# Moving one rotation behind a scaling and two low parts on VectorE in an attention kernel

## The reference, cut to what matters

```python
q = (x @ w_q); k = (x @ w_k); v = (x @ w_v)      # 32, 8 and 8 heads of 128
lq = x @ w_lq; lk = (lq @ w_lk); lv = (x @ w_lv) # 32 latent heads
q, k, lk = rope(q), rope(k), rope(lk)            # y * cos + rotate_half(y) * sin
attn = causal_softmax(q, repeat(k, 4)) @ repeat(v, 4)
lat  = causal_softmax(q, lk) @ lv
x = x + attn @ w_o + lat @ w_lo
x = x + ffn(layernorm(x))
```

## Time and profile before

| | us |
|---|---|
| median of 3 executions (lowest, highest) | 2121.59 (2121.29, 2122.29) |
| the profiled execution | 2121.26 |
| its span in the trace | 2119.5 |
| busy: TensorE, its weight loads | 2066.4, 1754.4 |
| busy: VectorE, ScalarE, GpSimd | 1531.2, 1203.0, 894.4 |

### The profile page before, as it was taken

The page is one execution under the profiler, slowest core; times in us unless marked ns, Lnnn a source line. Parts: engine busy times, 40 slices in busy tenths (PEclk is TensorE's granted clock), DMA queues, the critical chain, the costliest instruction groups (busy, mean ns, idle before and its releaser), DMA issues.

```text
span 2119.5 us, 32469 instructions
## 1 busy us (share of the span) xinstructions
PE 2066.4 (97%) x11236; PEld 1754.4 (83%) x11236; DVE 1531.2 (72%) x2946; ACT 1203.0 (57%) x2507; POOL 894.4 (42%) x691
## 2 busy tenths in 40 slices
PE   6999999999999999999999999999999999999989
PEld 5888888888888888888888888888888888888877
DVE  7777777776777677777677767777677777777775
ACT  4566555565566555566556555556646555555641
POOL 4433453444544353444443345444354345444411
PEclk9999999999999999999999999999999999999999
DMA  2111111111111111111111111111111111111121
GB/s 97 42 37 38 45 32 40 29 42 47 31 34 40 33 41 37 36 42 32 37 42 37 35 47 32 27 42 37 47 31 37 42 27 47 31 42 36 38 51 40
DMA packets 101937, 83.72 MB, mean 39 GB/s; under 512 B 28296, under 2 KB 73992, under 8 KB 101776
## 3 DMA queue, kind: packets, MB, share of 16 engines
q1 hardware_dynamic: 101776, 81.65, 15.1%
HBM read 79.26 MB, written 2.36 MB: 39 GB/s over the span
## 4 chain that ended last, share of the span: by engine, by line
PE 69%; DVE 15%; POOL 6%; issue 6%; ACT 4%; DMA 0%; SPq 0%; ACTq 0%; DVEq 0%
PE scores L433 9%; PE scores L435 9%; PE scores L434 9%; PE bankT L496 7%; PE bankX L433 6%; PE bankX L435 6%; PE bankX L434 6%; PE bankO L433 5%; PE bankO L435 5%; PE bankO L434 5%; DVE rot_half L1008 4%; DVE rot_half L1007 4%; DVE PT_lo L997 2%; POOL rot L1219 2%; POOL rot L1221 2%
## 5 line engine op out<-in xcount | busy, mean ns | idle before, releaser
L721 ACT ACTIVATE PT_hi<-bankT 128x512 fp32r<-128x512 f32 (+2 forms) x640 | 336.3, 532 | 389.1 <-PE bankO L435 326.9
L997 DVE TENSOR_TENSOR PT_lo<-bankT,PT_hi 128x512 fp32r<-128x512 f32 (+2 forms) x640 | 386.7, 607 | 194.7 <-ACT PT_hi L721 189.7
L780 ACT ACTIVATE probs<-probs,nmax 128x128 f32<-128x128 f32 (+7 forms) x512 | 395.5, 774 | 134.3 <-DVE nmax L991 133.7
L991 DVE CUSTOM_DVE_ANT_0 probs<-scores,mask 128x128 f32<-128x128 f32 (+7 forms) x512 | 381.3, 750 | 55.5 <-PE scores L435 54.4
L496 PE MATMUL bankT<-ident,probs 128*128 128x128 f32 x2304 | 379.1, 273 | 22.2 <-DVE PT_lo L997 20.0
L496 PEld LDWEIGHTS bankT<-ident,probs 128*128 128x128 f32 x2304 | 285.2, 140 | 90.6 <-DVE PT_lo L997 35.6
L1213 POOL TENSOR_TENSOR OT_lo<-o_raw,OT_hi 128x512 fp32r<-128x512 f32 x64 | 99.9, 1561 | 417.6 <-ACT OT_hi L721 417.6
L1219 POOL TENSOR_TENSOR rot<-rot,cos 128x512 f32<-128x512 f32 x144 | 186.2, 1293 | 199.4 <-DVE rot_half L1008 199.4
L721 ACT ACTIVATE OT_hi<-o_raw 128x512 fp32r<-128x512 f32 x128 | 147.0, 1148 | 145.5 <-DVE o_raw L1062 145.5
L1221 POOL TENSOR_TENSOR rot<-rot,rot_half 128x512 f32<-128x512 f32 x144 | 204.1, 1417 | 11.3
L1007 DVE TENSOR_TENSOR rot_half<-rot,sin 64x512 f32<-64x512 f32 x144 | 110.0, 764 | 85.4 <-ACT rot L721 81.7
(11 more groups left out here) (254 smaller groups left out, 5170.5 us busy)
## 6 DMA issues: line engine op xcount, KB each, us to landing
inv_b<-inverses SPq DMA_DIRECT2D x128, 256.0 KB, 3.9
stage<-in_L_attn_w_q SPq DMA_DIRECT2D x32, 256.0 KB, 4.8
stage<-in_L_attn_w_lv SPq DMA_DIRECT2D x32, 256.0 KB, 2.8
stage<-in_L_attn_w_o SPq DMA_DIRECT2D x32, 256.0 KB, 4.9
stage<-in_L_attn_w_lo SPq DMA_DIRECT2D x32, 256.0 KB, 2.6
acc<-in_L_attn_hidden_states SPq DMA_DIRECT2D x8, 256.0 KB, 4.8
stage<-in_L_attn_w_k SPq DMA_DIRECT2D x8, 256.0 KB, 5.1
stage<-in_L_attn_w_v SPq DMA_DIRECT2D x8, 256.0 KB, 5.4
```

The lines of the kernel that those rows point to most:

```text
L721: return act.activation(place, src, ACT.Copy)
L780: act.activation(prob_tile(c, t), prob_tile(c, t), ACT.Exp, bias=nmax[:, c, t:t + 1], scale=-1.0, accum_out=rsum[:, c, t:t + 1]).then_inc( ...
L991: dve.tensor_tensor_reduce(place, src, tile_view(mask[:, S - width:S], c), -SCALE, -MASKED, ALU.add, ALU.min, nmax[:, c, t:t + 1]).then_in ...
L997: dve.tensor_tensor(pt_place(1, hh, w, j), bankT[j % 2][:, block_columns(c, j):CH], f32(pt_place(0, hh, w, j)), ALU.subtract).then_inc(pt_ ...
```

## The change

The first half's rotation of the next queries, `("Q", 0)`, is taken out of step 3 of the third pass on VectorE, and is issued after the loop that holds the next pass's two low parts and the scaling, ahead of OT_lo. Its arguments and waits are the same. It applies to 31 heads. No other engine's order changes.

```diff
@@ -1086,7 +1086,7 @@
                         here = pieces_of(w, hh, more)
-                        if s in here and here[s][0] not in ("LK", "K"):
+                        if s in here and here[s][0] not in (("LK", "K", "Q") if w == 2 else ("LK", "K")):
                             piece(g, hh, w, s, *here[s], piece_bank(hh, w, s, more))
@@ -1101,6 +1101,8 @@
                             block_lo(g + 1, 0, 0, j)
+                    if w == 2 and more:
+                        rotate(rope_no(g, hh, "Q", 0), rope_no(0, hh, "Q", 0) % RING, 0)
                     if c == 0:
                         out_low(g, hh, w)
```

## The result

The changed kernel takes 2173.5 us (median; 2171.7 to 2174.2), against 2121.4 us before on the same chip: a ratio of 1.0245, 95% interval 1.0227 to 1.0263, 52 us slower. The profiled execution took 2173.15 us with a span of 2171.3.

A forecast was written before the change was run, and what follows sets the result against it. TensorE, busy for 97% of the span, was taken to bound the kernel with its own work plus waits. 2121.3 + 39.6 (1.65 us by 24 common heads) + 0 (group ends) = 2160.9, so 2161 us; range 2141 to 2181.

The forecast's parts named there:

- TensorE's single wait: Early in the fourth pass of a common head, TensorE waits once, for PT_lo, 0.5 us; added delay there isn't swallowed later.
- The part ahead of the rotation: VectorE's low parts and scaling start earlier, 716.32 instead of 717.24; OT_lo, behind the moved rotation, starts 0.26 us earlier.
- The turns: VectorE's OT_lo and second-half rotation alternate with GpSimd's two operations; low part of block 2 is 1.63 us late, 1.65 taken.
- QT_lo just in time: GpSimd's QT_lo is ready at 725.6, before TensorE's scores of the next queries need it at 726.0: 0.4 us slack.
- The group ends: At 7 group ends, a gain of the whole 1.05 us wait up to a loss: -7 to +12 us, taken as 0.
- The clock: Rival: longer stalls halve TensorE's clock, about 1.6 us a fall; 2199 us in all 24 heads, 2170 in a quarter; chance 0.12.
- full clock: Main case: VectorE and GpSimd take turns and TensorE's clock stays at 2.4 GHz; 2161 us, chance 0.76.
- As the order suggests: Rival: low parts come earlier and GpSimd doesn't hold VectorE up; some 11 us gained, 2110 us; chance 0.06.
- hidden: Rival: without collisions, later QT_lo cancels the common heads' gain, only group ends may gain; 2116 to 2122 us, chance 0.06.

The follow-up runs named there:

- e5: Old order plus one spare VectorE subtraction, reading one PSUM operand, ahead of the fourth pass's low part of block 2 in the 24 common heads (not last of a group): 2135.6 us.
- e6: Old order plus two spare VectorE subtractions, reading one PSUM operand, ahead of the fourth pass's low part of block 2 in 24 common heads: 2150.3 us.
- e7: Old order plus three spare VectorE subtractions, reading one PSUM operand, ahead of the fourth pass's low part of block 2 in 24 common heads: 2175.0 us.
- e3: Changed kernel with GpSimd's two operations on the first half of Q cut to 32 of 512 columns: 2111.4 us.
- e2: Old order, with the late rotation in the 7 group ends alone: 2121.7 us, ratio 1.0003.
- e9: Old order, fourth pass: rotation of Q's second half moved behind low part of block 3, ScalarE's first-half QT_hi ahead of PT_hi of block 3: 2098.0 us.
- e10: Old order with ScalarE's first-half QT_hi moved ahead of PT_hi of block 3, rotation of Q's second half left in place: 2159.1 us.
- e11: Changed kernel plus second-half Q rotation behind low part of block 3 and ScalarE's first-half QT_hi ahead of PT_hi of block 3: 2138.9 us.
- e1: Changed kernel with the late rotation kept only in the 24 heads not last of a group, group ends in old order: 2174.1 us.
- e8: Old order, with the fourth pass's rotation of Q's second half moved behind the low part of block 2: 2120.4 us.

## Why the prediction was right, point by point

**TensorE's single wait.** Right: whatever was added at this place passed through whole (e5, e6, e7), and the list of a common head has one entry before and after.

**The part ahead of the rotation.** Right: the low part left the rotation's wake. By the count, the rotation starts 1.82 us behind it; in the trace it is 1.92 (733.33 to 735.25). OT_lo had lost its own wait and came right behind.

**The turns.** Right in order and in size. The count had OT_lo first, the cosine at 2.2 us, L1007 at 1.55, the add at 1.6, L1008 at 1.7, and a low part 1.63 us late; the rows have 2.15, 1.54, 1.59, 1.67, and TensorE's wait is 1.59 us longer than in the earlier trace rows. e3 shows that these turns are the cause.

**QT_lo just in time.** Right: it ends at 742.61 and TensorE asks at 743.05, 0.44 us of slack where 0.4 was counted.

**The group ends.** Taken as 0, between -7 and +12 us; e2 has +0.0003 of the time, and its trace 0.5 us. The two halves of the argument both show: 0.2 us less for PT_lo, 0.3 more for QT_lo.

**The clock.** Here the size of the total was missed, 2161 against 2173.5. The measured time is inside the range, which had left room for a few falls; the 52 us are a third more than the 39.6 counted. The step that failed is the choice of full clock (0.76) over a falling one (0.12). The count had put the wait between one of 1.05 us that left the clock alone and one of 3.92 behind which it was halved, and then leant to the shorter side. Nine of 24 waits lowered it. The price of a fall was estimated at 1.6 us and is 1.5; a case in which a quarter of the heads are hit was put at 2170, and it was three eighths. The Trainium skill's page TensorE: Matmul & The Clock Gate (Part 1) has idleness lower the clock; that a stall this short would rather not was my reading of it, and the measurement decides against that.

**The rivals.** "As the order suggests" and "hidden" both needed VectorE and GpSimd to run side by side at that place, and they don't. e3 shows what the first would have given, 2111 us, where it had 2110. What "hidden" would have given no run shows, since in e3 QT_lo is early as well.

## What to carry to other kernels

Moving an instruction on an idle-looking engine moves its reader too: before the move, look at what its reader will do when it starts later, and on which memory. Two-operand SBUF work of VectorE and GpSimd that is issued at the same time goes in turns, so a chain of short instructions can pay one of GpSimd's for each of its own, as long as GpSimd has work queued; an order that lays GpSimd's work beside VectorE's reads from PSUM pays nothing for it (e9 has the same instructions as e10 and is 61 us faster). And when a wait of the bounding engine grows, count a second price if that engine's clock depends on being busy.

## What the runs showed of the hardware

**TensorE's clock fell behind waits of about 2 us.** Behind none of 24 waits of 1.7 us (e6), none of 24 of 1.11 (e5), none of 24 of 1.50 (e10) and none of the waits up to 1.7 in e11; behind 4 of 7 of 2.05 us (e10), 9 of 24 of 2.12 (the changed kernel, and e1 as well), and 6 of 24 of 2.30 (e7). In e1, e7 and e10 it also fell once near 50 us, behind two waits of 0.6 and 1.2 to 1.4 us that lie within 3 us of each other; the other kernels have these two waits, of 0.6 and 1.2 to 1.5 us, and no such fall. I had expected it only behind much longer ones. Each low stretch in the passes lasted 3.4 us and cost 1.5. In the changed kernel five of them lie 259 us apart (they begin at 617.7, 877.1, 1136.5, 1395.9 and 1655.3 us), in the first head of one group after the other. A low stretch doesn't begin at a fixed distance from its wait: in these traces it begins between 0.4 us ahead of the wait's end and 1.4 us behind it. Which waits are hit and which not was not tried, and stays open, as does why 2.30 us had fewer than 2.12.

**The turns are strict.** With two-operand SBUF work queued on both sides, neither engine got two in a row: VectorE's second half waited for the add although its first half had only just ended, and the add for the first half. In the passes of all 13 traces no such VectorE instruction lies wholly inside a GpSimd operation of 512 columns, nor the reverse, but for one that begins together with it (e8, at 974.34 us). A blocked GpSimd operation of 512 columns ended 1.11 to 1.16 us behind the end of the VectorE instruction ahead of it, a blocked half of the rotation 0.55 us behind GpSimd's end.
